# An eight-batch transformer block on one core: mixture two batches behind its attention, two attentions interleaved at the start, the last mixtures as one stream

## The reference, cut to what matters

```python
h = conv(x, cos(phases) * w_real - sin(phases) * w_imag)      # 16 taps, 750 rows in, 735 out
z = layernorm(h)
h = h + softmax(z @ Wq.T @ (z @ Wk.T).T / 8) @ z              # attention, one head
z = layernorm(h)
logits = z @ gate_w + gate_b                                  # 16 experts
w = softmax(top_2(logits))
moe = sum over the 2 chosen experts of w * (relu(z @ w1[e] + b1[e]) @ w2[e] + b2[e])
h = h + layernorm(z + moe) * gamma + beta
```

## Time and profile before

| what | value |
|---|---|
| time, median of 3 runs | 417.43 us (416.25 to 418.31) |
| the profiled execution | 413.8 us, with a span of 412.0 us and a mean granted clock of 0.993 |
| PE busy | 383.7 us, 93% of the span |
| DVE, ACT, POOL busy | 243.1, 173.2, 146.5 us (59%, 42%, 36%) |
| DMA | 55.93 MB, 136 GB/s on average |

### The profile page before, as it was taken

The page is one execution under the profiler, slowest core; times in us unless marked ns, Lnnn a source line. Parts: engine busy times, 40 slices in busy tenths (PEclk is TensorE's granted clock), DMA queues, the critical chain, the costliest instruction groups (busy, mean ns, idle before and its releaser), DMA issues.

```text
span 412.0 us, 6494 instructions
## 1 busy us (share of the span) xinstructions
PE 383.7 (93%) x2322; PEld 256.6 (62%) x2322; DVE 243.1 (59%) x579; ACT 173.2 (42%) x519; POOL 146.5 (36%) x167
## 2 busy tenths in 40 slices
PE   8987988999999999999999999999999989998992
PEld 6485578566775567566775667566766566455560
DVE  3265475565763677376663576277755764366793
ACT  3346433333554436434654345334653334331421
POOL 4100310055106631475108611565118601870241
PEclk9999999999999999999999999999999999999997
DMA  6500007900196006900295007800292029402930
GB/s 186 147 0 2 0 6 248 378 0 2 35 362 252 0 2 218 406 27 0 59 392 198 2 5 276 349 21 1 85 414 115 0 64 387 161 2 79 406 127 19
DMA packets 22847, 55.93 MB, mean 136 GB/s; under 512 B 3744, under 2 KB 4768, under 8 KB 22688
## 3 DMA queue, kind: packets, MB, share of 16 engines
q1 hardware_dynamic: 22816, 55.53, 36.1%
HBM read 53.57 MB, written 1.95 MB: 135 GB/s over the span
## 4 chain that ended last, share of the span: by engine, by line
PE 80%; DVE 12%; ACT 4%; issue 2%; DMA 1%; POOLq 0%; POOL 0%; ACTq 0%; DVEq 0%; SPq 0%
PE mix L913 22%; PE up L913 20%; PE small L913 17%; PE wide L913 14%; PE wide L939 3%; DVE row_max L739 3%; DVE hidden L801 2%; PE small L932 1%; PE wide L1012 1%; PE wide L1060 1%; ACT relu L540 1%; DVE xn L691 1%; DVE attn L748 1%; DVE cen L753 1%; ACT probs L548 1%
## 5 line engine op out<-in xcount | busy, mean ns | idle before, releaser
L801 DVE SCALAR_TENSOR_TENSOR hidden<-up,b_neg,gates_all 128x368 f32<-128x368 f32 x156 | 86.3, 594 | 30.0 <-PE up L913 29.9
L913 PE MATMUL up<-x,w_hi 128*128 128x368 f32 x230 | 86.5, 376 | 3.4 <-ACT relu L540 3.1
L913 PE MATMUL mix<-hidden,w2s 128*64 128x368 f32 x512 | 86.6, 478 | 0.3 <-DVE hidden L801 0.2
L309 POOL TENSOR_TENSOR hidden<-relu,gates_all 128x368 f32<-128x368 f32 x70 | 67.2, 992 | 55.2 <-ACT relu L540 46.1
L913 PE MATMUL up<-x,w_lo 128*128 128x368 f32 x230 | 75.8, 330 | 0.0
L426 POOL TENSOR_TENSOR rstd<-var_eps,power 128x6 f32<-128x6 f32 x24 | 31.9, 1331 | 111.9 <-ACT cen_sq L504 111.9
L540 ACT ACTIVATE relu<-up,b_pos 128x368 f32<-128x368 f32 x74 | 37.9, 564 | 73.1 <-PE up L913 73.1
L913 PEld LDWEIGHTS mix<-hidden,w2s 128*64 128x64 f32 x512 | 34.3, 136 | 43.8 <-issue 37.2
L913 PEld LDWEIGHTS up<-x,w_hi 128*128 128x128 f32 x230 | 43.2, 188 | 26.6 <-issue 9.1
L548 ACT ACTIVATE probs<-wide 128x736 f32<-128x736 f32 (+2 forms) x48 | 36.6, 779 | 24.3 <-PE wide L913 24.3
L739 DVE TENSOR_REDUCE row_max<-wide 128x1 f32<-128x736 f32 (+1 forms) x48 | 42.7, 915 | 1.7 <-PE wide L913 1.5
(11 more groups left out here) (137 smaller groups left out, 485.6 us busy)
## 6 DMA issues: line engine op xcount, KB each, us to landing
gates_all<-gates_far SPq DMA_DIRECT2D x128, 368.0 KB, 8.0
xt<-x_t SPq DMA_DIRECT2D x8, 375.0 KB, 11.3
out<-outs SPq DMA_DIRECT2D x8, 192.0 KB, 1.8
w_raw<-w SPq DMA_DIRECT2D x2, 512.0 KB, 6.3
w2s<-w SPq DMA_DIRECT2D x1, 512.0 KB, 7.4
gates_far<-gates_t SPq DMA_DIRECT2D x8, 46.0 KB, 1.7
gates_all<-w_real SPq DMA_DIRECT2D x1, 256.0 KB, 2.6
gates_all<-w_imag SPq DMA_DIRECT2D x1, 256.0 KB, 2.8
```

The source lines that it names most:

```text
L309: eng.tensor_tensor(hidden[:, e % HIDDEN, s, :], relu[:, pooled_index(n, e) % 2, s, :], gates_all[:, e, s * HALF:(s + 1) * HALF], ALU.mult ...
L801: dve.scalar_tensor_tensor(hidden[:, e % HIDDEN, s, :], up_of(n, e, tail)[s], b1_neg[:, e:e + 1], gates_all[:, e, s * HALF:(s + 1) * HALF] ...
L913: return pe.matmul(dst, lhsT, rhs, start=start, stop=stop, skip_group_check=True)
```

## The change

It changes neither a tile's size nor an operation's shape. It changes the order on all five engines:

- Mixture m = i - 2 runs in iteration i (before: m = i - 1). `h1`, `xn2` and `x2` get a third buffer, `gates` a second.
- The opening does attention 0 and 1 interleaved and the first scores of batch 2, with convolutions 2 and 3 cut into pieces between them in the bank `mix`; of the `keep_awake` products only the first 14 stay. Several copies of the opening move from ACT to DVE (the `shift` of batch 1, one copy of the keys of batch 1, the keys and the token copy of batch 2, the second features of batch 0). No mixture runs in it.
- Iteration 2 is the first and iteration 7 the last. After the attention sum of batch 7, `last_mixtures` runs the experts 4 to 15 of batch 5 and all of batches 6 and 7 in groups of four (`first_layers`, `second_layers`), over the three bank pairs and ten `hidden` buffers, six of them in `probs`.
- For batches 6 and 7 no expert is pooled: DVE's `hide` does all. That needs a second bias matrix (`bias_all`), 16 products more.

```diff
+def is_pooled(n, e):
+    return n < DENSE and e in POOLED
...
+def freed_by(n, e):
+    return E * n + e - (RING if ending(n, e) else HIDDEN)
...
             opening()
-            for i in range(1, BATCH + 1):
-                iteration(i, i % 2, i == 1, i < BATCH, i < BATCH - 1, i < BATCH - 2)
+            for i in range(AHEAD, BATCH):
+                iteration(i, i % 2, i == AHEAD, i < BATCH - 1, i < BATCH - 2)
...
             def query_hi(n):
                 act.wait_ge(s_q, n + 1)
-                copy(split(q_hi[:]), wide[query_buf(n)][:, :, 0:HALF]).then_inc(s_qhi, 1)
+                act.wait_ge(s_score, NT * n)
+                copy(split(q_hi[:]), query_home(n)[:, :, 0:HALF]).then_inc(s_qhi, 1)
...
             def opening():
+                variance(0, cen0[1], 1)
                 shift(0)
-                exponentials(0, 0, NT)
-                variance(0, cen0[1], 1)
+                keys_hi(1)
+                exponentials(0, 0, NT - 1)
+                query_hi(1)
+                exponentials(0, NT - 1, NT)
+                conv_copy(2, mix)
                 attention_copy(0)
                 variance(1, cen1, 0)
-                keys_hi(1)
-                keys_hi_again(1)
...
+                exponentials(1, 0, 2)
                 variance(0, cen0[0], 2)
+                exponentials(1, 2, NT)
...
             def opening():
-                for t in range(NT):
-                    max_scores(0, t, 1 - t % 2, t - 1)
-                    keep_awake(2)
-                pe.wait_ge(s_moe_in, 16 * MOE_LOADS)
...
+                for t in range(NT):
+                    max_scores(0, t, 1 - t % 2, t - 1)
+                convolve(2, 0, 3, 6, mix)
                 transpose_max(0)
-                for t in range(NT):
+                pe.wait_ge(s_ln[0], 2)
+                pe.wait_ge(s_h0, 2)
+                to_features(up_pair, xn1[1], s_t1)
+                for t in range(4):
                     scores(0, t)
+                project(1)
+                for t in range(4, NT):
+                    scores(0, t)
+                convolve(2, 0, 6, CHUNKS, mix)
+                for t in range(4):
+                    pe.wait_ge(s_prob, min(t + 5, NT))
+                    max_scores(1, t, 1 - t % 2, t - 1)
                 for t in range(NT):
                     weigh_values(0, t, 0)
...
-                gate_logits(0, 0)
-                max_scores(1, 0, 0, 0)
-                pe.wait_ge(s_biasw, 1)
-                keep_awake(4)
-                pe.wait_ge(s_logit, 1)
-                keep_awake(6)
-                pe.wait_ge(s_gap, 1)
-                keep_awake(6)
-                transpose_gates(0)
...
+            def last_mixtures(i):
+                pe.wait_ge(s_prob, NT * i + NT)
+                transpose_gates(LONG + 1)
+                first_layer(LONG, 4)
+                attention_to_tokens(i)
+                first_layer(LONG, 5)
+                pe.wait_ge(s_gtc, LONG + 2)
+                first_layer(LONG, 6)
+                first_layer(LONG, 7)
+                second_layers(LONG, 0)
+                first_layers(LONG, 8)
...
+                m = LONG + 1
+                first_layers(m, 0)
+                second_layers(LONG, 12)
+                first_layers(m, 4)
+                pe.wait_ge(s_hid, hidden_before(m, 5, 1, False))
+                transpose_gates(m + 1)
+                gated_biases(m)
+                second_layers(m, 0)
+                pe.wait_ge(s_gtc, m + 2)
+                first_layers(m, 8)
...
```

More of the change, by code:

```diff
@@ L164, in build @@
         pick = sb("pick", [P, 2, NT, E])
-        gates = sb("gates", [P, NT, E])
+        gates = [sb(f"gates_{k}", [P, NT, E]) for k in range(2)]
         gates_t = sb("gates_t", [E, TOKP])
@@ L438, in gamma_beta, with second_norm, first_sum @@
                 pool.tensor_tensor(outs[:], res[2][:], h1[buf][:], ALU.add).then_inc(s_res, 1)
-            def iteration(i, par, first, att, conv, ahead):
-                if conv and not first:
+            def second_norm(n):
+                pool.wait_ge(s_ftc, CREDIT + n + 1)
+                pool.tensor_tensor(cen2[:, :, 0:D], moe_tok[:], xn2[n % 3][:, :, 0:D], ALU.add).then_inc(s_cen[2], 1)
+                deviation(2, n)
+                gamma_beta(n, n % 3)
+            def first_sum(i):
+                pool.wait_ge(s_attn, i + 1)
+                pool.tensor_tensor(h1[i % 3][:], attn[:], h0[i % 2][:], ALU.add).then_inc(s_h1, 1)
@@ L442, in iteration @@
+            def iteration(i, par, first, conv, ahead):
+                if conv:
                     deviation(0, i + 1)
                 if not first:
[L444 to L450, removed]
-                                       ALU.add).then_inc(s_fin, 1)
-                    deviation(2, BATCH - 1)
-                    return
+                    second_norm(i - 3)
@@ L776, in gate @@
                 g = 8 * i
+                at, wsum, wtop, second = gate_room(i)
                 dve.wait_ge(s_topi, NT * i + NT)
@@ L805, in hide_both @@
-            def hide_both(n, e, att):
-                if e not in POOLED:
-                    hide(n, e, 0, not att)
-                    hide(n, e, 1, not att)
-                elif not att:
-                    gate_hidden(dve, n, e)
-            def last_hidden():
-                for e in range(SPLIT, E):
-                    hide_both(BATCH - 2, e, False)
-                for e in range(E):
-                    hide_both(BATCH - 1, e, False)
-            def iteration(i, par, first, att, conv, ahead):
-                m, before = i - 1, i - 2
-                if not att:
-                    last_hidden()
-                    return
+                dve.tensor_tensor(gates[i % 2][:], pick[:, 0, :, :], second, ALU.add).then_inc(s_gates, 1)
@@ L823, in iteration, with next_max, second_normed @@
+            def next_max(i, t):
+                reduce_max(i + 1, t, MAX_BUF[t])
+            def second_normed(i):
+                if i >= 3:
+                    dve.wait_ge(s_cen[2], CREDIT + i - 2)
+                normalise(1, xn2[i % 3], cen1, i)
+            def iteration(i, par, first, conv, ahead):
+                m, before = i - 2, i - 3
                 if conv and not first:
@@ L1158, in iteration @@
                 if not first:
-                    for e in range(SPLIT, E):
-                        second_layer(before, e)
-                first_layer(m, 0, buf)
+                    second_layers(before, SPLIT)
+                    first_layer(m, 0)
                 scores(i, 3)
-                first_layer(m, 1, buf)
+                if not first:
+                    first_layer(m, 1)
                 if conv:
```

641 lines of the change are left out of this document (387 added, 254 removed).

## The result

The changed kernel took 410.82 us (median of 4 runs, 408.21 to 411.34), the kernel before 416.84 beside it (415.72 to 418.31): ratio 0.985, 95% interval 0.982 to 0.989. It is faster, as forecast, and within the range of 400 to 411.5, but by 6.0 us at the medians, where 12.1 had been forecast, and above the 403 to 408.5 that had been given 0.60. The profiled execution took 410.4, with a span of 408.5, where the sum had 399.9 and before 412.0.

The account below looks back on a forecast made before the run. PE work was taken to bound steady iterations, leaving slack only in the opening and around attention 7. From 412.0, +12.4 +2.8 -45.6 +18.3 gave 399.9; 12.1 off the median 417.4 gave 405.3 us, range 400 to 411.5.

Parts of the forecast that it names:

- the sum: Whole kernel: profiled 412.0 plus 12.4 opening, plus 2.8 iteration 2, minus 45.6 for one iteration, plus 18.3 end: 399.9 us.
- rival 2: End stream: bound by buffers or DVE, each group of four losing 0.5, 11 groups 5.5, time 411 us; chance 0.08.
- Weighing the clock: the sum keeps the full clock: Opening without most keep_awake products: PE busy some 6 of 9 us at its thinnest, clock taken to stay full.
- The fourth rival: Opening from about 48 us: the clock falls to 1.2 GHz, up to 20 us more, time 425 us; chance 0.04.
- The opening: Up to iteration 2's start: two interleaved attentions, ending at 78.1 us, 12.4 later than iteration 1 started before.
- The walk: Opening: every step timed with trace durations and hand-overs of 0.02 to 0.15 us, putting iteration 2's start at 78.1.
- rival 1: Opening: slower than walked through some missed wait, iteration 2 at 83 to 86, time 411 us; chance 0.16.
- the sign of it: Opening forecast wrong if PE waits for probs, q_lo or row_max more than 15 us in total before 78.
- Iteration 2: Old iteration 1 (40.5 us) plus batch 1's transposes, logits and gates and some DVE steps: 43.3 us, +2.8.
- The end stream: Behind iteration 7's attention: 11 groups of first layers, 12 of second, and extras: 70.6 us against 52.3, +18.3.
- my 1.5: Start of the end stream: 1.5 us added for its first three experts' waits and ACT's copy of 16 gate rows.
- The base: Starting time: 12.1 taken off the median 417.4, not the profiled 413.8, which was 3.6 below it: 405.3 us.

Follow-up runs that it names:

- before_filled: Kernel before the change, with six identity products added in each of PE's two waits around attention 7: 416.66 us, ratio 0.999.
- The edits of this part: Changed kernel with filled waits, plus convolution taps between row maxima, or batch 1's last two maxima earlier, or both: 405.20, 407.70, 407.03 us; both mended, with eight more products: 405.90.

## Why the prediction was right or wrong

**Direction and mechanism: right.** One steady iteration goes (136.8 for three, 45.6 each to 0.1), its experts come back at the end at the predicted 5.51 for a group of four, and the second attention costs less in the opening than in an iteration. That DVE and the hidden buffers do not bound the stream was right as well (rival 2): the chain there is PE on PE, and DVE waits 1.4 to 2.8 for PE per group.

**"Weighing the clock: the sum keeps the full clock": this step failed.** It cost 4.5 to 4.7 of the 8.6. I had read one row, 30 to 40 with PE busy 7.14 at a clock of 1.00, as what the chip does at that load. before_filled, which is the same program up to there, shows that stretch at half clock, so the row was one of two draws. The fourth rival named the mechanism and the starting place within 10 us, but priced it as one long drop of up to 20 us. What happens is three short ones, of some 5, 4 and 4 us, worth 1.5, 1.6 and 1.5, the third not in the opening but in iteration 7. The Trainium skill, in TensorE: Matmul & The Clock Gate, section HAM oscillation, was right in kind: the clock does fall to half where bursts of matmuls have waits between them. This trace agrees on the fall, from 0.17 to 0.30 between matmuls at 38.19, behind waits of 0.2 to 0.9. It does not agree that each wait has this effect: the section's own case has far longer waits, for DMAs, and here waits of 1.35 and 1.30 in iteration 2 passed at a clock of 1.00 from 60 to 110 us. I set its rule aside on the strength of one row.

**The opening: mis-sized by 2.0** beyond the clock (79.9 to 80.2 with the waits filled, forecast 78.1). The walk's order of waits was right, but its steps were short by some tenths each, and these add up: the row maxima of batch 1 at 41.4 (40.7), the scores at 53.0 (51.7), tile 3 at 57.8 (56.4), the projection of batch 2 at 65.0 (63.0). By its numbers rival 1 came true, with iteration 2 at 83.34 and a time of 410.8 for its 83 to 86 and 411, but not by its cause: 3.1 of the opening's 5.2 are the clock, and no single wait was missed. PE's waits for `probs`, `q_lo` and `row_max` from 23 to 78 add up to some 6 us, far from the 15 that were to be the sign of it. So it is partly luck that the time lies within the range, whose upper end was set by rivals 1 and 2 and left the clock out. The edits of this part shortened it by 0.6 at most, since two chains of nearly equal length meet at the features of batch 0.

**Iteration 2: +0.9 over the forecast.** PE waits 1.35 for the keys of batch 3 and 1.30 for a row maximum; the same waits of iteration 1 are 0.56 and 0.25 in before_filled. I had 0.6 for the DVE steps ahead of the row maxima, and nothing for the keys, which cost 0.8 more.

**The end stream: +0.9.** The waits in it are 0.30, 0.25, 1.10 and 0.28, together 1.9 for my 1.5. The largest stands before experts 12 to 15, which need `wide[1]` back from ACT's and DVE's x2 copies: DVE's ends at 344.04, PE goes on at 344.14. ACT's stands behind two rectifications, before which ACT waits 2.47 for POOL. What makes up the rest I did not take apart.

**The base: an error that hid another.** I set the sum against the profiled execution and subtracted the difference from the median, as if the 3.6 between them stayed. Mostly they are the clock that the kernel before loses at 33, 2.8 in before_filled. The changed kernel's profile and median are 0.4 apart. So the sum was 8.7 too low, the base 3.2 too high for it, and the forecast missed by 5.5.

## What to carry to other kernels

Before you take filler products out of a kernel, cost them as clock, not as idle time, and try them in the new waits, no longer than the wait. A single profile of a stretch with waits doesn't tell the clock there: compare its time with the median of the runs, and where they differ by more than the spread, ask which stage took the difference. And in an opening with several chains, look for the second chain before you shorten the first.

## What the hardware showed that I had not expected

- The clock falls behind short waits. In the changed kernel it halved at 38.19 with no wait above 0.9 since 30; in the kernel before at 32.8 behind waits of 0.72 and 0.86 in one trace, and not at all in another of the same program up to there. By their times and mean clocks most executions beside two groups had such a drop, and fewer beside the first.
- Identity products in these waits, 19 of them and 12 more between the maxima, gave 1.2% (410.8 to 405.7, on two chips; 408.5 to 403.8 by the spans). The kernel before lost 2.0% without its own.
- A turn between first and second layers costs 0.36 with both its sides, without a wait in the trace.
